# Two neighbours per query gathered by query, the rest through one 128-edge unit per tile, in fp32

## What is computed

```python
def layer(x, adjacency, Wq, Wk, Wv):
    q, k, v = x @ Wq.T, x @ Wk.T, x @ Wv.T
    mask = adjacency.T
    scores = where(mask, q @ k.T, -1e30)
    attn = where(mask, softmax(scores, axis=1), 0)
    return attn @ v
x = layernorm(x + layer(x, adj, L0...))
x = layernorm(x + layer(x, adj, L1...))
```

## Time and profile before

| | |
|---|---|
| runs of the kernel | 298.88, 301.24, 304.02 us (median 301.24) |
| profiled execution, span | 300.1 us |
| mean granted clock of PE | 0.844 of full speed |
| busy: PE, DVE, ACT, POOL | 205.3, 175.3, 103.1, 99.6 us |

### The profile page before, as it was taken

The page is one execution under the profiler, slowest core; times in us unless marked ns, Lnnn a source line. Parts: engine busy times, 40 slices in busy tenths (PEclk is TensorE's granted clock), DMA queues, the critical chain, the costliest instruction groups (busy, mean ns, idle before and its releaser), DMA issues.

```text
span 300.1 us, 5513 instructions
## 1 busy us (share of the span) xinstructions
PE 205.3 (68%) x1854; PEld 171.6 (57%) x1854; DVE 175.3 (58%) x974; ACT 103.1 (34%) x285; POOL 99.6 (33%) x118
## 2 busy tenths in 40 slices
PE   1898758645108799679999968404398684999860
PEld 1777635424007678568998736202277573888750
DVE  0859986761015466556878961301315575799995
ACT  1034579500103353544565321200333322344510
POOL 4000000577742565361000007777116665220000
PEclk9999995975555999998999977855569999699996
DMA  6992000133330323231111123344103343231112
GB/s 247 365 365 77 0 3 1 42 101 105 96 79 20 88 70 107 70 102 42 37 36 38 35 70 78 101 105 103 37 2 87 82 118 84 72 87 38 35 40 73
DMA packets 14815, 25.04 MB, mean 83 GB/s; under 512 B 1984, under 2 KB 9664, under 8 KB 14784
## 3 DMA queue, kind: packets, MB, share of 16 engines
q0 software_dynamic: 4608, 12.59, 16.6%
q1 hardware_dynamic: 10176, 12.06, 11.8%
HBM read 20.45 MB, written 4.19 MB: 82 GB/s over the span
## 4 chain that ended last, share of the span: by engine, by line
PE 41%; DVE 17%; issue 15%; another core or an unknown queue 13%; ACT 9%; DMA 3%; DVEq 0%; SPq 0%
PE PS L844 11%; PE PS L927 10%; PE PS L937 5%; PE PS L915 5%; DVE prod L621 4%; ACT Q L338 3%; DMA adj_words<-in_adj 3%; DVE near L663 2%; PE PS L836 2%; ACT dist L345 2%; DVE X L681 2%; PE PS L820 2%; PE PS L852 2%; PE PS L981 1%
## 5 line engine op out<-in xcount | busy, mean ns | idle before, releaser
L296 POOL DMA_INDIRECT xg<-in_x,key_row x48 | 48.3, 1007 | 84.1 <-DVE key_row L582 51.1
L296 POOL DMA_INDIRECT xg<-x_rows,key_row x48 | 47.9, 997 | 80.3 <-DMA x_rows<-X 43.9
L621 DVE CUSTOM_DVE_ANT_0 prod<-PS,xg 128x256 f32<-128x256 f32 x96 | 38.8, 420 | 46.0 <-remote 20.9
L927 PE MATMUL PS<-weight,xg 128*128 128x128 f32 x384 | 52.2, 290 | 14.9 <-ACT weight L397 14.9
L927 PEld LDWEIGHTS PS<-weight,xg 128*128 128x128 f32 x384 | 49.9, 206 | 16.3 <-ACT weight L397 15.6
L915 PE MATMUL PS<-Q,own 128*128 128x256 bf16 x288 | 45.4, 316 | 1.2 <-issue 1.0
L844 PE MATMUL PS<-M,xt 128*128 128x256 f32 x104 | 30.2, 441 | 15.5 <-ACT xt L360 8.9
L915 PEld LDWEIGHTS PS<-Q,own 128*128 128x128 f16 x288 | 30.5, 112 | 8.1 <-issue 1.1
L937 PE MATMUL PS<-WvT,y_sb 128*128 128x256 f32 x128 | 31.0, 385 | 5.6 <-ACT y_sb L370 3.2
L844 PEld LDWEIGHTS PS<-M,xt 128*128 128x128 f32 x104 | 21.6, 218 | 20.6 <-ACT xt L360 9.9
L397 ACT ACTIVATE weight<-own_t,prob 128x128 f32<-128x128 f16 x96 | 29.8, 389 | 0.5
(11 more groups left out here) (130 smaller groups left out, 291.2 us busy)
## 6 DMA issues: line engine op xcount, KB each, us to landing
adj_words<-in_adj SPq DMA_DIRECT2D x4, 1024.0 KB, 10.5
X<-in_x SPq DMA_DIRECT2D x2, 1024.0 KB, 12.2
x_rows<-X SPq DMA_DIRECT2D x8, 256.0 KB
out<-X SPq DMA_DIRECT2D x8, 256.0 KB
xg<-in_x,key_row POOLq DMA_INDIRECT x48
xg<-x_rows,key_row POOLq DMA_INDIRECT x48
W<-in_L_gnn_Wq SPq DMA_DIRECT2D x2, 256.0 KB, 8.9
W<-in_L_gnn_Wk SPq DMA_DIRECT2D x2, 256.0 KB, 7.5
```

Of the source, the lines that this page charges most:

```text
L296: pool.indirect_dma_start(xg[:, t % RING, n, :], None, rows, bass.IndirectOffsetOnAxis(ap=key_row[:, t, n:n + 1], axis=0), bounds_check=N ...
L621: dve.tensor_tensor_reduce(out=prod[:, i // U, n, :], in0=expanded(i // U, n), in1=xg[:, t % RING, n, :], op0=ALU.mult, op1=ALU.add, scale ...
L927: last = nc.tensor.matmul(PS[:, 5, at_h:at_h + P], xg[:, t % RING, n, h * P:h * P + P], weight[:, t % 2, n, :], start=(n == 0), stop=(n == ...
```

## The change

- **Lists.** A query's first two neighbours (S = 2) are taken straight from the two largest words (`direct_rows`), for 4 tiles of queries as soon as their block of the adjacency is packed; the adjacency therefore is loaded in blocks of 4 tiles of *queries* (512 bytes in a row). The other neighbours (`overflow_codes`) go through an edge list of one unit of 128 edges a tile, made for 8 tiles at a time.
- **Gathers.** Still three units of 128 rows a tile: two by query into `xd`, one by edge into `xo`. Both hold all 16 tiles, so no gather waits for a buffer. POOL's order is: direct 0 to 7, (listed 1) overflow 0 to 7, direct 8 to 15, (listed 2) overflow 8 to 15; in layer 1 all 48 after one wait.
- **Arithmetic.** Q, own, own_t and the scores are fp32 and the splitting into bf16 parts is gone with `less`. `expand` is one fp32 matmul a tile; the products of the direct slots read Q itself in SBUF.
- **Order.** ACT makes four direct weights (identity scaled by the exponent) between the exponents and the overflow weights, and the last step of the norm moves from DVE to ACT (`normal`). PE runs `sums(p)` in step p and `projected(p)` at the head of step p+1. PE enters the loop after "listed" 2.

```diff
             def adjacency(c):
-                sp.dma_start(adj_words[:, 4 * c:4 * c + 4, :],
-                             adj[512 * c:512 * c + 512, :].rearrange("(t p) n -> p t n", p=P)).then_inc(a_in[c], 16)
+                at_q = c * QT * P // 4
+                sp.dma_start(adj_words[:, :, at_q:at_q + QT * P // 4],
+                             adj[:, at_q:at_q + QT * P // 4].rearrange("(t p) n -> p t n", p=P)).then_inc(a_in[c], 16)
...
-                for t in range(T):
-                    if layer == 0 and t % (T // LISTS) == 0:
-                        pool.wait_ge(s["listed"], t // (T // LISTS) + 1)
-                    need(pool, "y_ready", t + layer * T - RING + 1)
-                    for n in range(U):
-                        pool.indirect_dma_start(xg[:, t % RING, n, :], None, rows,
...
+            for h in range(HALVES):
+                for c in (2 * h, 2 * h + 1):
+                    pool.wait_ge(s["directs"], c + 1)
+                    for t in range(QT * c, QT * c + QT):
+                        direct(x, t)
+                pool.wait_ge(s["listed"], h + 1)
+                for t in range(HT * h, HT * h + HT):
+                    overflow(x, t)
+            pool.wait_ge(s["x1_stored"], 16 * PAIRS)
+            for t in range(T):
+                direct(x1_dram, t)
+                overflow(x1_dram, t)
...
+            direct_rows(0)
+            direct_rows(1)
+            overflow_codes(0)
+            direct_rows(2)
+            starts(0)
+            direct_rows(3)
+            ownership(0)
+            what_edges_get(0)
+            overflow_codes(1)
+            starts(1)
+            ownership(1)
+            what_edges_get(1)
...
+            pack_part(0)
+            product(0, 4)
+            transposes(X0, 0)
+            transposes(X0, 1)
+            queries(0)
+            pack_part(1)
+            transposes(X0, 2)
+            queries(1)
+            transposes(X0, 3)
+            queries(2)
+            pack_part(2)
+            queries(3)
+            pack_part(3)
...
+                expand(layer, 0)
+                for p in range(PAIRS + 3):
+                    if layer == 0 and among(p - 3):
+                        pe.wait_ge(s["normed"], 2 * (p - 3) + 2)
+                        transposes(X1, PAIRS + p - 3)
+                    if among(p - 1):
+                        projected(layer, p - 1)
+                    if among(p):
+                        scatter(layer, p)
+                        tops_of_edges(layer, p)
+                    if among(p + 1):
+                        expand(layer, p + 1)
+                    if layer == 0 and among(p - 3):
+                        queries(PAIRS + p - 3)
+                    if among(p):
+                        sums(layer, p)
...
+                    if among(p):
+                        exponents(layer, p)
+                        direct_weights(layer, p)
+                    if layer == 0 and among(p - 3):
+                        queries(PAIRS + p - 3)
+                    if among(p):
+                        overflow_weights(layer, p)
+                    if among(p - 2):
+                        normal(layer, p - 2)
+                    if among(p):
+                        summed(layer, p)
```

More of the change, by code:

```diff
@@ new lines, in overflow_weights @@
+            def overflow_weights(layer, p):
+                n = layer * PAIRS + p
+                act.wait_ge(s["ds_ready"], n + 1)
+                act.activation(prob[:, n % 2, :], shifted[:, n % 2, :], ACT.Exp, scale=-1.0).then_inc(s["p_ready"], 1)
+                act.wait_ge(s["p_ready"], n + 1)
+                for j in range(2):
+                    act.activation(weight[:, n % 2, j, S, :], own_t[:, 2 * p + j, :], ACT.Copy,
+                                   scale=prob[:, n % 2, j:j + 1]).then_inc(s["a_ready"], 1)
@@ new lines, in overflow_codes @@
+                chain(dve.tensor_tensor(third[:, tiles, :], rest, second_p, ALU.subtract))
+                chained()
+                chain(dve.scalar_tensor_tensor(out=codes[:, :, KW - S:2 * KW - S], in0=rest, scalar=float(NW), in1=code2,
+                                               op0=ALU.is_ge, op1=ALU.mult))
+                chained()
+                listed = codes[:, :, 0:2 * KW - S]
+                for t in range(HT):
+                    chain(dve.max(nbr[:, HT * h + t, 0:8], listed[:, t, :]))
@@ new lines, in overflow_codes @@
+                chained()
+                for t in range(HT):
+                    chain(dve.match_replace(out=listed[:, t, :], in_to_replace=nbr[:, HT * h + t, 0:8],
+                                            in_values=listed[:, t, :], imm_value=0.0))
+                chained()
+                for t in range(HT):
+                    chain(dve.max(nbr[:, HT * h + t, 8:16], listed[:, t, :]))
+                chained()
+                chain(dve.tensor_scalar(held[:, :, :], nbr[:, tiles, :], 0.0, None, ALU.is_gt))
@@ L931, in projected, with offsets @@
[L931 to L934 removed]
+            def offsets(h):
+                tiles = slice(HT * h, HT * h + HT)
+                pe.wait_ge(s["counted"], h + 1)
+                nc.tensor.matmul(PS[:, 4 + h, 0:HT], before[:, :], n_over[:, tiles], start=True, stop=True)
+                nc.tensor.matmul(PS[:, 4 + h, HT:2 * HT], ones[:, :], n_over[:, tiles], start=True,
+                                 stop=True).then_inc(s["off_ps"], 1)
```

1003 lines of the change are left out of this document (446 added, 557 removed).

## The result

| | before | after |
|---|---|---|
| median (fewest to most) | 302.63 us (298.88 to 304.09) | 354.01 us (352.25 to 355.52) |
| profiled execution, span | 300.1 us | 353.8 us |
| mean granted clock of PE | 0.844 | 0.777 |
| busy: PE, DVE, ACT, POOL | 205.3, 175.3, 103.1, 99.6 us | 210.2, 142.0, 97.5, 99.4 us |

The changed kernel is slower by 18%: the ratio is 1.180, with a 95% interval of 1.171 to 1.190. Some executions of a kernel are a few per cent slower than its others; ratios, and medians from here on, leave them out (before: 300.1 us), but the traces of e1_land_pair, e1_again, h1_before_landed and i1_gap are of such executions, and only waits and distances are read from them. The forecast was 316 us with a range up to 334: the sign was right and the size was not. The span is 38 us above the forecast.

A forecast was written before the change was run, and what follows sets the result against it. Bound: PE hand-offs late by 5 to 16 us in unbroken gather streams, then one chain per pair. First sums 97, layer 0's pairs and 12 to 182, stream and tail to 247, pair 1 249, six pairs 304, end 316 us; range 302 to 332.

The forecast's parts named there:

- The hand-offs in the stream: Layer 1's unbroken gathers: each PE hand-off takes 5 to 10 us, so 5 to 10 deliveries in 50 us.
- rival 3: Queries wait in layer 0's first stream too, only pair 0 done in layer 1's stream: 337 us, slower by 12%; chance 0.10.
- "Listed" 2: Layer 0's second half of the lists: ready at 84 us, behind the stream's end; 66 to 70 without lateness.
- "Listed" 1: Layer 0's first half of the lists: taken at 50 us, between 46 and 55; POOL then issues 24 gathers, to 81.
- The first sums: Layer 0: the first sums end at 97 us, against 94.3 before; bounds 75 and 109.
- the pairs of layer 0: Layer 0's loop: pairs 1 and 2 at 9.1 us each, pairs 3 to 7 at 10.9 us each.
- I count nothing: DVE loses some 2 us a pair, ACT gains two normalizations; both have slack in 9.1 us, so 0 us.
- Six pairs x 9.1: Layer 1 behind pair 1's sums at 249 us: six pairs of 9.1, 54.6 us, to 304.
- Rival 1: Stalls are no matter of the gather streams: first sums at 75, layer 1's first gather at 160, end 253 us; chance 0.20.
- Rival 4: Shorter work wins back the stream: pairs run at 7.5 us instead of 9.1, 303 us, no change; chance 0.12.
- Rivals 1 and 2: The second of them: hand-offs late but less so, one in 3 us, 289 us, faster by 4%; chance 0.16.
- The rule on descriptors: DVE's two-port fp32 operations block GpSimd's gather descriptors: 7 us more in layer 0's preamble, left out of the sum.

The follow-up runs named there:

- e1_land_pair: Changed kernel; in layer 1 POOL waits, before each pair's six gathers, for the landing of the pair before: 276.3 us (chip 0), 278.7 (chip 11), 309.7 (chip 5).
- h1_before_landed: Kernel before; in both layers POOL waits, before each pair of tiles, for the landing of the pair before: 290.7 us beside 302.5, ratio 0.965 (chip 5).
- i1_gap: Changed kernel; in layer 1 POOL sets memory once and waits for itself before each pair's six gathers, for no landing: 305.2 us beside 302.5, ratio 1.015 (chip 5).
- the two other orders: Changed kernel, chip 3: ACT's overflow weights ahead of layer 1's queries, 337.2 us; or PE's scatter ahead of projection and DVE's top ahead of residual, 336.0 us.

## Why the prediction was wrong

Its structure stood: that the last lists come behind the end of layer 0's long stream, that the stream of layer 1 is unbroken for 62.5 us (measured 62.5), that it decides, and that the loop behind it is longer than before. The 38 us come in three lots, measured against the sum's unrounded terms (first gather of layer 1 at 181.7, pair 1's sums at 249.2, end at 315.8).

**1. The hand-offs in the stream, the step that failed.** "Before got one through in about 10 us in such a stream; I let it be 5 to 10." The copy of pair 0's sums needs two increments, one a tile, both made by 215.64; the trace's semaphore records have them arrive at 240.8 and 264.6. In the second trace of the changed kernel increments arrive at 226.3, 246.0 and 264.2. The traces of the two other orders have them at 218.5 and 245.2, and at 221.2 and 247.1. The arrivals at 264 are no rate: they come 5 us behind the last gather. So behind the prompt part only one or two increments arrive within the stream, the first 12 to 27 us after it was made and a second 20 to 27 us behind the first, where I had 5 to 10 us for each and 5 to 10 of them. The 10 us of the earlier trace rows was no rate. The first of those two waits did end inside the stream, but I counted it from its instruction's end: between arrivals of PE's increments (190.34 and 203.16) it was 12.8 us; the second one (10.53 us) ended 3.2 us behind the last gather, where the ring stops POOL. A wait that the end of the stream cut short was read as the delay of one delivery. Pair 1's sums therefore came 80.3 us after the first gather and not 67.5: 12.8 us. My rival 3 names it, "once the delay grows with the stream's length"; but I priced it at one pair more, 337 us. Whether the delay does grow with the stream, or is 12 to 27 us from the start, these few arrivals don't tell.

**2. Layer 0, 15.1 us.** "Listed" 2 was taken at 84, at the end of the stream. "Listed" 1 came at 56.4, where I took 50, just outside my bounds of 46 to 55: DVE had stood for 12.6 us (until 23.4) and 10.0 us (until 50.3) waiting for PE, whose packing had its breaks beside the first two streams. On chip 11, where it has none, POOL could go on at 40.6. So the stream moved from 81 to 88.3; the lists came 3 us behind that, and were ready at 93. The first sums ended at 105.96 and not at 97 (the bounds were 75 and 109). Two more terms are in this lot: the pairs of layer 0 took 9.3 and 11.3 us, where 9.1 and 10.9 were forecast, 2.9 us in all; and 15.2 us, not 12, passed from the last sums to the first gather. The chain shows the pair's last norm step, which the change moved to ACT, behind the copy of the last queries:

```profile
192.27 0.60 ACT Q L338
192.87 0.98 ACT X L419 x2
193.87 2.12 DMA x_rows<-X
```

I had written "I count nothing" for it.

**3. The end, 10.2 us.** "Six pairs x 9.1" became 63.8 us, and the end 13.0 and not 12. Two of the pairs took 9.3. Three took 10.7 to 10.9, where the granted clock was at its lower level during the sums, which I hadn't reckoned with behind the stream, and the pair behind the flag 12.9:

```profile
317.11 0.60 ACT L410 ACTIVATE y_sb<-PS 128x512 f32<-128x512 f32 x1 [3.24 <-PE PS L956]
317.23 0.16 DVE L739 CAST over_i<-PS 128x1 int32<-128x1 f32 x1 [5.35 <-PE PS L993]
...
330.03 0.60 ACT L410 ACTIVATE y_sb<-PS 128x512 f32<-128x512 f32 x1 [3.91 <-PE PS L956]
```

PE makes the flag behind the sums of step 5, and DVE waits for it before anything of step 6. It took 12.9 us where the pairs at the lower clock took 10.7 to 10.9: the flag costs about 2 us. On chip 11 it was 11.45 us against 9.26 of the fastest pairs, at a mean granted clock of 0.85 in it.

**The rivals.** Rival 1 (253 us) was a true account of the other kind of chip, up to its loop: on chip 11 the first sums were copied at 74.7 (forecast 75), layer 1's first gather came at 164.1 (160), and the end at 268.9. The 16 us over 253 are these 4, 3 to pair 0's sums, 8 in the seven pairs (10.2 us each with half clock and flag, not 9.1) and 1 at the end. That it would be faster than before was wrong, since the kernel before gains 58 us there as well. Rival 4, pairs at 7.5, was refuted on every chip: in no run of the new loop did several pairs follow each other faster than 9.0 us (single ones took 7.4 and 8.0). Rivals 1 and 2 had 0.36 of the chance together and no share in the result.

**The rule on descriptors.** I had put 7 us on a rule of the Trainium skill that would have slowed the gathers beside DVE's decoding ("SBUF — State Buffer", on DVE's two-port operations), and left it out of the sum. The 32 direct gathers of layer 0, most of them beside DVE's decoding, took 1005 ns in the mean, those of layer 1 with DVE idle beside most of them 1001: it is not seen here, and leaving it out was right.

## What to carry to other kernels

A wait that ends together with the thing that causes it gives no rate: before a delay is extrapolated, find out what ended it, here POOL's stream, and price the longer stream by its whole length. Where POOL issues indirect gathers in a long unbroken row, a pause of 2 us after every six, or a wait for the landing (8 us where it wasn't needed), leaves waits of at most 6 us for the sums in the place of 34 to 52. A ring buffer that looks like a brake can be what lets the other engines through; and a measured gain or loss can belong to one kind of chip, so a change is judged best on more than one.

## What the hardware showed that was not expected

- **Hand-offs of PE are held while POOL issues indirect gathers, by up to 49 us** in the first measurements, 30 to 46 us on chip 3, and not at all on chips 0 and 11, with the same program; none was held in the first 12 us of layer 1's stream. PE's own packing matmuls, which wait for nothing, are held as well, from 6 to 7 us into a stream. ACT's were hardly ever late; some of DVE's by 1 to 3 us. On chip 5 plain loads by POOL (26 us of them) and memory sets (46 us) hold nothing back, and with a pause of 1.75 us after six gathers no wait for the sums is over 5.6 us. Whether it takes the recording of the execution as well is open.
- The end of a matmul in the trace is a modelled one. The Trainium skill says so too, and that PE's update is sent only once PSUM has acknowledged the writes ("Perfetto Trace Analysis", on the matmul instruction). So it isn't shown whether the increment is held, or the last write to PSUM, or, as the breaks in the packing suggest, all that PE completes; no run here tells these apart.
- **The clock follows the stall**: in slices 26 to 30, in which PE had nothing to do, and in 31 behind them, the granted clock is 5 tenths, and the projection behind the stall takes 3.78 us where it takes 1.99 at the higher level. A stall is paid twice.
